# Attention row sums on Trainium2: the first two key tiles of a unit are added by an accumulating transfer as well

## The reference

```python
h = _rmsnorm(x, g1) * (1.0 + scale1[:, None, :]) + shift1[:, None, :]
x = x + _mha(h, w_qkv, b_qkv, w_ao, b_ao, n_head)
h = _rmsnorm(x, g2) * (1.0 + scale2[:, None, :]) + shift2[:, None, :]
x = x + _ffn(h, w_fc, b_fc, w_fo, b_fo)
...
# in _mha, after the rotation of q and k:
attn = jnp.einsum('bhqd,bhkd->bhqk', q, k) * (1.0 / np.sqrt(hd))
attn = jax.nn.softmax(attn, axis=-1)
out = jnp.einsum('bhqk,bhkd->bhqd', attn, v)
```

## Time and profile before

| | |
|---|---|
| time, median of 3 runs | 3583.11 us (3581.57 to 3583.68) |
| the profiled execution's own time | 3584.84 us |
| its span, first to last instruction | 3583.0 us |
| PE busy | 3218.5 us (90%) |
| DVE busy | 2025.6 us (57%) |
| ACT busy | 1572.8 us (44%) |
| POOL busy | 1665.3 us (46%) |
| DMA, mean over the span | 142 GB/s |
| granted TensorE clock, mean | 0.941 of full speed |

### The profile page before, as it was taken

How to read it: one execution, slowest core, us unless ns; L and a number is a source line. 1 busy time by engine, 2 the same in 40 slices (tenths; PEclk the granted TensorE clock), 3 DMA queues, 4 the chain that set the end, 5 groups by cost and what they waited for, 6 DMA issues and landing times. The chain is left out here.

```text
span 3583.0 us, 53307 instructions
## 1 busy us (share of the span) xinstructions
PE 3218.5 (90%) x15180; PEld 2074.7 (58%) x15180; DVE 2025.6 (57%) x3254; ACT 1572.8 (44%) x2848; POOL 1665.3 (46%) x732
## 2 busy tenths in 40 slices
PE   5888789999999999999999994433999998999999
PEld 5666644444444444444444442432888886788887
DVE  2887677878777876878787783533322221322222
ACT  1333217676677766777676773233211111211111
POOL 0222318888788887888788886554100000100000
PEclk9999859999999999999999997766999999999999
DMA  4444449898898988899798987554411211411210
GB/s 168 141 141 142 134 91 194 179 195 189 165 196 183 194 176 171 181 188 199 160 194 178 193 191 166 170 182 161 144 47 47 94 47 49 143 66 47 94 47 24
DMA packets 179320, 508.04 MB, mean 142 GB/s; under 512 B 25914, under 2 KB 43434, under 8 KB 145966
## 3 DMA queue, kind: packets, MB, share of 16 engines
q0 software_dynamic: 36240, 248.53, 34.2%
q1 hardware_dynamic: 132308, 233.59, 21.7%
q10 hardware_dynamic: 10512, 22.81, 1.9%
HBM read 175.18 MB, written 93.62 MB: 75 GB/s over the span
## 5 line engine op out<-in xcount | busy, mean ns | idle before, releaser
L733 DVE TENSOR_REDUCE b_mpart<-b_m 128x1 f32<-128x512 f32 x2136 | 1325.9, 685 | 385.2 <-PE b_m L783 381.3
L672 ACT ACTIVATE b_pt<-b_s 128x512 f32<-128x512 f32 x2048 | 1115.0, 596 | 522.3 <-PE b_s L808 466.4
L711 POOL TENSOR_TENSOR b_acc<-b_acc,b_pt 128x2048 f32<-128x2048 f32 x225 | 1049.2, 4663 | 204.9 <-DMA b_pt<-b_pt 204.2
L808 PE MATMUL b_s<-b_qs,b_ks 98*128 98x512 f32 x2050 | 890.9, 435 | 23.7 <-ACT b_pt L672 23.7
L783 PE MATMUL b_m<-b_ks,b_qs 96*128 96x512 f32 x2136 | 787.2, 415 | 20.5 <-issue 20.2
L808 PEld LDWEIGHTS b_s<-b_qs,b_ks 98*128 98x128 f32 x2050 | 387.3, 189 | 675.3 <-ACT b_pt L672 617.5
L860 PE MATMUL b_o<-b_pt,b_vg 128*32 128x512 f32 x4096 | 549.5, 609 | 0.0
L783 PEld LDWEIGHTS b_m<-b_ks,b_qs 96*128 96x128 f32 x2136 | 417.6, 196 | 96.2 <-DVE b_mpart L733 26.3
L1245 DVE SCALAR_TENSOR_TENSOR d_uf<-d_a,keep_chan,d_sg 128x512 f32<-128x512 f32 x128 | 96.1, 751 | 578.1 <-PE d_a L1273 578.1
L1197 POOL DMA_DIRECT2D d_raw<-in_w_fc x32 | 24.0, 755 | 591.7 <-POOLq L1122 495.7
L1216 ACT ACTIVATE d_sg<-d_g,keep_chan 128x512 f32<-128x512 f32 x128 | 88.1, 689 | 419.7 <-PE d_g L1273 419.7
(11 more groups left out here) (130 smaller groups left out, 3606.6 us busy)
## 6 DMA issues: line engine op xcount, KB each, us to landing
b_pt<-b_pt POOLq DMA_DIRECT2D x225, 1024.0 KB, 8.1
b_ks<-scratch_qk_hi SPq DMA_DIRECT2D x36, 512.0 KB, 5.6
b_qs<-scratch_qk_hi SPq DMA_DIRECT2D x68, 256.0 KB, 5.5
scratch_qk_hi<-a_q_hi SPq DMA_DIRECT2D x64, 256.0 KB, 2.5
scratch_qk_lo<-a_q_lo SPq DMA_DIRECT2D x64, 256.0 KB, 2.8
d_h_hi<-scratch_h_hi SPq DMA_DIRECT2D x16, 1024.0 KB, 7.4
d_h_lo<-scratch_h_lo SPq DMA_DIRECT2D x16, 1024.0 KB, 9.6
d_y<-scratch_y SPq DMA_DIRECT2D x16, 1024.0 KB, 8.0
```

What stands on the lines that cost most here:

```text
L672: act.activation(pt[:, kt % RING, h, :], ps_s[:, i % LEAD, :], ACT.Exp, scale=SCALE).then_inc(p_ready, 1)
L711: pool.tensor_tensor(acc[slot][:], acc[slot][:], pt[:, (2 * n + 3) % RING, :, :], ALU.add).then_inc(pool_added, 1)
L733: dve.tensor_reduce(mpart[slot][:, i // 4, i % 4:i % 4 + 1], ps_m[:, i % EARLY, :], AX.X, ALU.max).then_inc(max_done, 1)
L808: pe.matmul(ps_s[:, i % LEAD, :], ks[kslot][0:QR, h, kt * P:(kt + 1) * P], qs[qslot][0:QR, h, :], start=True, stop=True).then_inc(st_done, 1)
```

## The change

The pair (0, 1) becomes an ordinary pair: a transfer adds tile 0 onto tile 1, so that there are 8 transfers and 7 additions a unit instead of 7 and 8. `first_pair` is gone. The pairs are numbered from 0 again, pair `n` being tiles `2n` and `2n + 1`. The first addition of a unit takes tile 1's slot (which holds 0 + 1) and tile 3's slot (2 + 3) and writes `acc`; so slot 1 stays in use until the pair (2, 3) has landed and been added, and tile 9, which overwrites it, waits for that (`added(v, max(old // 2, 1))`). Tile 8 waits for the landing of pair 0. POOL's order becomes: transfer 0, the last addition of the unit before, transfer 1, a wait for the landing of pair 0, transfer 2, addition 1, transfer 3, addition 2, and so on to transfer 7, addition 6.

```diff
-PAIRS = NK // 2 - 1
-ADDS = PAIRS + 1
+PAIRS = NK // 2
+ADDS = PAIRS - 1
...
-            return ADDS * u + ADDS + (n + 3 if n < PAIRS - 1 else 2 + ADDS)
+            return ADDS * u + ADDS + (n + 1 if n < PAIRS - 1 else 1 + ADDS)
+
+        def landed(u, n):
+
+            return 16 * (PAIRS // 2 * u + n // 2 + 1 + n % 2)
...
                 old = (kt - RING) % NK
-                if old >= 2 and old % 2 == 0:
-                    g = PAIRS * (j if kt >= RING else j - 1) + old // 2 - 1
-                    if g >= 0:
-                        act.wait_ge(pair_in[g % 2], 16 * (PAIRS * 4 * pair + g // 2 + 1 + g % 2))
-                    else:
-                        act.wait_ge(pool_added, added(u - 1, old // 2 - 1))
-                elif old >= 2:
-                    act.wait_ge(pool_added, added(u if kt >= RING else u - 1, old // 2 - 1))
+                v = u if kt >= RING else u - 1
+                if old % 2 == 0 and (kt >= RING or j):
+                    act.wait_ge(pair_in[old // 2 % 2], landed(v, old // 2))
                 else:
-                    act.wait_ge(pool_added, ADDS * u + ADDS + 1)
+                    act.wait_ge(pool_added, added(v, max(old // 2, 1)))
...
-            def first_pair(u, slot):
-
-                pool.wait_ge(p_ready, STEPS * (u + 1) + GH * 2)
-                pool.wait_ge(d_ps, u + 1)
-                pool.tensor_tensor(acc[slot][:], pt[:, 0, :, :], pt[:, 1, :, :], ALU.add).then_inc(pool_added, 1)
+            def fold_pair(u, n):
+
+                kt = 2 * n + 1
                 pool.wait_ge(pv_done, NK * u + RING - 1 + kt + 1)
                 pool.nop(nofuse=True)
+                pool.dma_start(pt[:, kt % RING, :, :], pt[:, (kt - 1) % RING, :, :], accum_op=ALU.add).then_inc(pair_in[n % 2], 16)
...
+            def add_pair(u, n, slot):
+
+                pool.wait_ge(pair_in[n % 2], landed(u, n))
+                if n == 1:
+                    pool.wait_ge(d_ps, u + 1)
+                    first = pt[:, 1, :, :]
+                else:
+                    pool.wait_ge(pool_added, added(u, n) - 1)
+                    first = acc[slot][:]
+                pool.tensor_tensor(acc[slot][:], first, pt[:, (2 * n + 1) % RING, :, :], ALU.add).then_inc(pool_added, 1)
 
             def body(u, pair, j):
-                first_pair(u, j % 2)
-                fold_pair(u, j, pair, 0)
-                add_pair(u - 1, j - 1, pair, PAIRS - 1, (j + 1) % 2)
-                for n in range(1, PAIRS):
-                    fold_pair(u, j, pair, n)
-                    add_pair(u, j, pair, n - 1, j % 2)
+                fold_pair(u, 0)
+                add_pair(u - 1, PAIRS - 1, (j + 1) % 2)
+                fold_pair(u, 1)
+                pool.wait_ge(pair_in[0], landed(u, 0))
+                for n in range(2, PAIRS):
+                    fold_pair(u, n)
+                    add_pair(u, n - 1, j % 2)
```

More of the change, by code:

```diff
@@ L691, in _ @@
             pool.sem_inc(pool_added, ADDS)
-            def first_pair(u, slot):
-                pool.wait_ge(p_ready, STEPS * (u + 1) + GH * 2)
-                pool.wait_ge(d_ps, u + 1)
-                pool.tensor_tensor(acc[slot][:], pt[:, 0, :, :], pt[:, 1, :, :], ALU.add).then_inc(pool_added, 1)
-            def fold_pair(u, j, pair, n):
-                kt = 2 * n + 3
+            def fold_pair(u, n):
+                kt = 2 * n + 1
                 pool.wait_ge(pv_done, NK * u + RING - 1 + kt + 1)
@@ L703, in fold_pair @@
                 pool.nop(nofuse=True)
[L704 to L711, removed]
@@ L721, in _ @@
+            def body(u, pair, j):
+                fold_pair(u, 0)
[5 more added lines that the diff above has]
+                    add_pair(u, n - 1, j % 2)
             run(pool, body)
-            pool.sem_inc(pool_added, 1)
-            add_pair(UNITS - 1, 7, UNITS // 8 - 1, PAIRS - 1, 1)
+            add_pair(UNITS - 1, PAIRS - 1, 1)
```

## The result

| | before | after |
|---|---|---|
| median of the runs, us | 3583.19 | 3693.51 (4 runs, 3686.58 to 3702.38) |
| ratio | | 1.0313, 95% interval 1.0297 to 1.0330 |
| profiled execution, us | 3584.84 | 3702.38 |
| its span, us | 3583.0 | 3700.6 |
| PE busy, us | 3218.5 | 3261.6 |

The change makes the kernel 3.1% slower, 110 us. The prediction was 3610, slower, with a range up to 3645: the sign was right, the size far too small. The two profiled spans differ by 117.6 us.

What follows compares the result with a forecast made beforehand. PE was taken to bound the kernel at 50.76 us a unit, POOL's chain close behind. Profiled 3584.84 + 32 (lateness) - 7 (waits gone) + 2 (clock) = 3611.8 us, median 1.7 lower: 3610, range 3578 to 3645.

Steps and rivals of the forecast that it cites:

- What bounds the kernel, and which wait: Stage B: PE sets 50.76 us a unit, POOL's chain is second; new ACT waits before tile 9, 20 to 50 us.
- the deadline of 15.1 us with 3.2 to spare: Before tile 9: the first addition may end 15.1 us after tile 3's transfer; its link takes 11.9, so 3.2 are free.
- POOL's work: On POOL: 32 additions, 147.6 us, go, busy lower by some 120 us; worth 0 by itself beside PE's work.
- The lateness that grows by 1.5 us a unit: POOL's odd chain takes 52.3 us a unit, 1.5 over PE's period; lateness gathers through each iteration, 32 us lost.
- Interference: Tile 1's transfer could lengthen tile 3's landing from 7.2 to at most 10.1 us; taken as 0, at most 81.
- Rival C: The DMA engines become the bound, share 1.03 in unit 9; landings 1 us longer give 3666 us; chance 0.13.
- my two signs for C: In stage B: ACT waiting for landings rather than additions, or median landings over 9 us, would show the DMA engines bind.
- The clock: PE's granted clock may fall after the new waits of about 1.5 us; 2 us taken, bounds 0 and 84.
- The gain: At iteration starts the waits before tile 6 go: 7.3 us won, the upper bound; lower bound 0.
- The sum: Whole kernel: 3584.84 + 32 - 7 + 2 = 3611.8 us profiled; the median 1.7 lower, 3610.

Runs made afterwards that it cites:

- hold_only: Kernel before, with only tile 9 made to wait until pair (2, 3) has been added, as in the changed kernel: 3579.99 us, 1.0003.
- third_ahead: Changed kernel with tile 3's transfer issued ahead of the last addition of the unit before, and four semaphores instead of two: 3687.07 us, 1.0304.
- first_tiny: Changed kernel with tile 1's transfer cut from 1 MB to 16 KB and a bias in ACT's copy of the denominators: 3673.02 us, 1.0265.
- ahead_tiny: Changed kernel with tile 3's transfer ahead of the last addition and tile 1's transfer cut to 16 KB, with the bias: 3575.15 us, 0.9984.
- hold_land45: Kernel before, with tile 9 made to wait also for the landing of tiles 4 and 5, which it doesn't need: 3597.89 us, 1.0050.
- j0_order: Kernel before, with the last addition of the unit before put ahead of tile 3's transfer at `j == 0` only: 3576.21 us, 0.9997.
- first_small: Changed kernel with tile 1's transfer cut to 16 KB and an added VectorE instruction in place of the bias: 3679.10 us, 1.0273.
- queries_late: Changed kernel with the query loads moved to after tile 4 and the first two key pieces to after tiles 4 and 7: 3795.76 us, 1.0601.

## Why the prediction was right in sign and wrong in size

- **What bounds the kernel, and which wait.** Right. PE sets the period, the chain of POOL and its transfers is the second, and the new waits are ACT's for POOL's first addition before tile 9, 87.7 us of them where I expected 20 to 50. `hold_only` shows the deadline of 15.1 us with 3.2 to spare to be harmless with the old chain.
- **POOL's work.** Right: 257 transfers, 225 additions, busy 123.3 us lower (120 predicted), worth nothing by itself.
- **The lateness that grows by 1.5 us a unit: the step that failed first.** I had 2.2, 3.7, 5.2 ... 11.2 us in an iteration. In the trace, tile 15's transfer is 1.1 us late on average and 3.7 at most, before the change 1.0 and 2.7: nothing gathers. Where units lose time they lose 7 to 9 us already in the second of an iteration, and two units later almost nothing is lost. A slip that PE has to wait off moves all of PE's later releases too, and so the chain has gained on it; that explains why no unit inherits it. The lateness is made anew at each turn, by one link: tile 3's transfer stands behind tile 15's landing (10 to 12 us) and addition. I had counted that link, but too small: 2.2 us late after the first turn, under the 3.2 that are free, so without any loss; the trace has 4.2 to 6.5 us in the second units of the four iterations, and 3.6 on average behind the first unit of an iteration. At the turn to unit 9 it is 4.3: tile 15's transfer was itself 1.6 late, which I had left out of the first turn, and landed in 10.6 instead of 10.1.
- **Interference, taken as 0 (bounds 0 and 81): the term that was mis-sized.** Tile 3's landing went from 7.4 to 9.4 on average, 12.2 where the transfer is kept on time. The reason I gave was that the DMA engines had a gap between tile 15's transfer and tile 3's, and that two transfers go out 6 us apart and take 5.2 each. The gap is not there. The stretch that counts begins with tile 15's transfer and ends when the addition of tiles 2 and 3 must begin, 15.1 - 4.74 = 10.4 us after PE lets tile 3's transfer go. This is that stretch at unit 9 of the kernel before, the changed kernel and `third_ahead` (columns of the earlier trace rows; the DMA share is the last but one):

```profile
986.22:1008.04 21.82, 21.82 (x115) 10.67 (x113) 17.32 (x29) 15.26 (x29) 18.26 (x8) 1.00 0.94 207
1017.94:1039.34 21.40, 21.40 (x113) 10.47 (x112) 16.88 (x28) 14.88 (x29) 12.49 (x7) 1.00 1.03 222
1009.57:1031.36 21.79, 21.79 (x115) 10.66 (x113) 17.28 (x29) 15.24 (x29) 12.62 (x7) 1.00 1.01 229
```

  Before, the engines were already busy for 0.94 of it; that could have been read before the change was run, and it leaves some 1.3 us for a transfer that takes 5.2. After, they are full (0.84 in `first_tiny`, 0.97 in `ahead_tiny`). What was asked of them can be estimated: from the earlier trace rows the stretch is 12.6 + 15.1 - 4.74 = 23 us. In it fall three transfers where two were, 3 × 5.2 = 15.6 us of all engines; queries and stored output, 1 MB by their sizes, some 5; and in three units of four one or two pieces of 512 KB, 2.5 each: 20.6 us in a unit without, 23 to 25.6 with. The packets of `third_ahead`'s trace bear it out. Added up from tile 15's transfer to tile 3's landing, queue 0 takes 16 to 18 us of all engines in every unit behind the first of an iteration, and SP's queue 4.0 to 4.4 in units without pieces, 6.7 to 7.0 with value pieces and 8.0 to 8.4 with key pieces (means by place in the iteration). `ahead_tiny` (5 us less work, and the order of before) loses nothing at tile 9. Where 23 us of room meet 23 to 26 of work, taking away the lateness of 4 us is no help by itself; and where the order makes tile 3 late, one transfer less is none: that is the table with two ways to miss.
- **Rival C** was right in mechanism and got only 0.13. I asked whether the share of the DMA engines over a whole unit passes 1, and reckoned 1.03 for unit 9. It stays at 0.90 to 0.97 in the windows above, but these have grown: 0.93 of 57.5 us is 53 us of work, over PE's period of 50.76. What C lacked is where in the unit the work falls: in the 23 us of a turn the demand passes what is there also in units whose mean is lower. One of my two signs for C, a median landing over 9 us, is there (9.2); the other, ACT waiting for landings, is not.
- **The clock: 2 us taken, bounds 0 and 84, measured 43.1.** I took short waits of 1.5 us, and for such `hold_land45` shows that the clock hardly costs (5.2 us for 14 waits). But of the 25 waits at tile 9 in the changed kernel 19 bring half clock: all 18 in which PE idles 2.25 to 6.35 us, and one of 1.75; the others, of 1.85 us and less, do not. The size of the wait was wrong, and the price hung on it: 43.1 us for 19 drops is 2.3 each, where the upper bound had 3.0.
- **The gain: 7.3.** Right: 7.3 us lost before tiles 6 and 7 before, none after. That reordering these at `j == 0` gives the same without the change is what `j0_order` suggests, unproven.
- **The sum.** 32 became 80 (123.5 less 43.1), 2 became 43, -7 held: 116, against 27 predicted.

By the page "DMA: Bandwidth & Descriptors" of the Trainium skill, section Queues, rings and completion order, a DMA engine goes round-robin between its queues, a packet at a time. The traces agree so far as they can. In `third_ahead`, between the landings of tiles 1 and 3 (1028.05 to 1035.14), the packets of queue 0 take 5.2 us of all engines, one transfer's worth, and those of SP's queue 2.2, although SP asked for its key piece at 1026.79, 5.9 us after tile 3's transfer went out. So a later load on another queue lengthens a transfer. Tile 5's transfer, issued at 1028.68 on the same queue, took nothing of that. And 8 KB transfers of the maxima beside pieces of 512 KB take 5.5 us instead of 1.7. Whether the turns are by packet the traces do not show.

What stays open: what the changed kernel would take without the query loads. The packets tell how much of the engines' time these and the pieces use, but no run took the query loads away.

## What to carry to other kernels

Where an operation is moved to a transfer, don't compare its time with the mean share of the DMA engines: draw the stretch between the transfer that releases the chain and the next deadline, and add up everything that other queues put into it; here that stretch of some 22 us was already 0.94 full, and the change put 5 us more into it. A share that stays under 1 afterwards proves nothing where the stretch it is taken over has grown. In a pipelined body, what goes out behind the last operation of the turn before inherits its lateness at every turn, so look at the order at the turn first, but expect no cure from it where the engines are full. And price a new wait twice, once as idle time and once as slow matmuls behind it: here 0.5 to 0.6 us for each us of waiting where PE mostly idled 2 to 7 us at a time, and 5 us for 14 waits where it idled 2.0 us at most.

## What the runs showed of the hardware

- A small VectorE instruction can wait for a whole GpSimd addition. In `first_small`, `tensor_scalar` on 128x16 took 3.67 us, and the reciprocal on the same tile 0.25; it ended at 679.90, as the addition on POOL did at 679.87. Of the 33 executions of this instruction, 11 start while an addition runs; all 11 last until it ends, 3.3 to 4.5 us. The other 22 take 0.16 to 0.23 us.

```profile
676.23 3.67 DVE L745 TENSOR_SCALAR b_dcol<-b_dcol 128x16 f32<-128x16 f32 x1
679.94 0.25 DVE L747 RECIPROCAL b_dcol<-b_dcol 128x16 f32<-128x16 f32 x1
```

```profile
675.31 4.56 POOL L709 TENSOR_TENSOR b_acc<-b_acc,b_pt 128x2048 f32<-128x2048 f32 x1 [0.36 <-DMA b_pt<-b_pt]
```

  The page "SBUF — State Buffer" of the Trainium skill (section SBUF: two separate sides) says that VectorE, in some of its modes, and GpSimd hold a common pair of ports for the length of an instruction while the other stands. The trace agrees; which mode this instruction ran in it doesn't show.
- An accumulating transfer of 1 MB within SBUF lands in 6.9 us at best, in 7.4 with room and in up to 19.5 us when queries and key pieces come at the same time (`queries_late`).
- The granted clock was 0.50 from 1047.2 to 1054.1 in the changed kernel; it fell while PE idled for 4.46 us (until 1049.17) and rose again after PE had been at work for 4.9 us. In the same kernel it fell in all 18 idle times of 2.25 us and more at tile 9 and in one of 1.75, and not in those of 1.78 and 1.85; in `hold_land45` it fell in one of 1.67 and not in one of 2.00. Idle time alone does not say when it falls.
